# Routed experts after attention: scatters straight from six input tiles at ten a turn, expert codes counted once from a table, and fresh units from batch 13

## The reference, cut to what matters

```
x = x + cross_attention(layernorm(x), ctx)            # 16 heads of 8
z = layernorm(x)
scores = sigmoid(z @ gate_w.T) + gate_bias            # 64 experts in 8 groups
keep the 4 groups with the largest maxima, then the 6 largest scores, weights divided by their sum
routed = sum over the 6 of weight * down_e(silu(gate_e(z)) * up_e(z))     # inner width 64
shared = one expert of inner width 128, for every token
out = x + shared + routed
```

## Time and profile before

| what | value |
|---|---|
| runs | 802.83, 805.97, 804.34 us |
| span of the profiled execution | 792.4 us |
| median of the runs less that span | 11.9 us (launch and end; the profiled execution's own time is not listed) |
| PE busy | 503.3 us, 64% |
| DVE busy | 456.1 us, 58% |
| POOL busy | 389.3 us, 49% |
| ACT busy | 352.3 us, 44% |
| granted PE clock, mean | 0.675 of full speed |

### The profile page before, as it was taken

The page is one execution under the profiler, slowest core; times in us unless marked ns, Lnnn a source line. Parts: engine busy times, 40 slices in busy tenths (PEclk is TensorE's granted clock), DMA queues, the critical chain, the costliest instruction groups (busy, mean ns, idle before and its releaser), DMA issues.

```text
span 792.4 us, 12061 instructions
## 1 busy us (share of the span) xinstructions
PE 503.3 (64%) x3204; PEld 420.8 (53%) x3204; DVE 456.1 (58%) x2264; ACT 352.3 (44%) x962; POOL 389.3 (49%) x425
## 2 busy tenths in 40 slices
PE   3767555766555574632359956788688889777700
PEld 2445334444334343311359856778688789777700
DVE  6587556667555576656233624576776756346532
ACT  3564433344443343322215934466666766246400
POOL 2006445654455655556650055454554545555574
PEclk9885555555555555555568976899988876897555
DMA  7532123322123332223425533455455555654421
GB/s 195 194 113 94 62 100 107 104 100 98 47 80 107 107 100 98 95 78 129 124 81 134 148 94 95 106 138 151 126 145 137 151 137 146 160 153 107 113 70 47
DMA packets 98708, 90.60 MB, mean 114 GB/s; under 512 B 10576, under 2 KB 85456, under 8 KB 98640
## 3 DMA queue, kind: packets, MB, share of 16 engines
q1 hardware_dynamic: 85232, 64.26, 27.5%
q0 software_dynamic: 12288, 25.29, 11.3%
q10 hardware_dynamic: 1120, 0.28, 0.2%
HBM read 41.32 MB, written 48.46 MB: 113 GB/s over the span
## 4 chain that ended last, share of the span: by engine, by line
PE 30%; another core or an unknown queue 17%; issue 16%; ACT 14%; POOL 11%; DVE 9%; ACTq 2%; DMA 0%; POOLq 0%; DVEq 0%
PE bank_s L1155 14%; POOL pages L447 6%; PE bank_o L1155 4%; PE bank_q L1155 3%; PE bank_s L1151 2%; ACT d_now L511 2%; ACT p_t L533 2%; ACT pxt L511 2%; POOL empty L492 2%; ACT gu_now L511 2%; ACT k_exp L521 1%; ACT s_act L672 1%; POOL p_t L492 1%; PE bank_o L1151 1%
## 5 line engine op out<-in xcount | busy, mean ns | idle before, releaser
L1155 PE MATMUL bank_s<-pxt,gu_now 128*128 128x64 f32 x768 | 116.5, 316 | 51.6 <-ACT pxt L511 31.3
L492 POOL DMA_INDIRECT p_t<-results,place_i x96 | 91.1, 949 | 110.6 <-ACT s_act L672 72.8
L1155 PEld LDWEIGHTS bank_s<-pxt,gu_now 128*128 128x128 f32 x768 | 111.4, 231 | 58.1 <-ACT pxt L511 36.4
L492 POOL DMA_INDIRECT empty<-results,place_i x96 | 91.1, 949 | 77.2 <-issue 35.1
L1111 DVE TENSOR_TENSOR h_t<-bank_s,s_act 64x256 f32<-64x256 f32 x128 | 54.7, 427 | 113.9 <-ACT s_act L672 95.4
L447 POOL DMA_INDIRECT pages<-payload,place_i x96 | 93.0, 968 | 37.9 <-issue 27.0
L447 POOL DMA_INDIRECT pages<-payload_b,place_i x96 | 92.8, 967 | 35.8 <-issue 26.7
L437 POOL TENSOR_TENSOR rstd<-ve,minus_half 128x4 f32<-128x4 f32 (+1 forms) x21 | 18.6, 885 | 132.6 <-DVE ve L927 130.0
L672 ACT ACTIVATE s_act<-bank_s 64x512 f32<-64x512 f32 x64 | 37.8, 590 | 79.5 <-remote 36.0
L533 ACT ACTIVATE p_t<-bank_s 128x512 f32<-128x512 f32 x64 | 36.2, 598 | 67.9 <-issue 27.9
L1255 PE MATMUL bank_o<-bias_h,row_h 96*128 96x256 bf16 x16 | 6.1, 381 | 72.2 <-ACT o_t L511 70.3
(11 more groups left out here) (169 smaller groups left out, 1164.1 us busy)
## 6 DMA issues: line engine op xcount, KB each, us to landing
pg<-pages SPq DMA_DIRECT2D x64, 258.0 KB
results<-y_s SPq DMA_DIRECT2D x64, 256.0 KB
pages<-empty SPq DMA_DIRECT2D x21, 774.0 KB
w_gu<-in_expert_gu SPq DMA_DIRECT2D x16, 256.0 KB
w_d<-in_expert_d SPq DMA_DIRECT2D x31, 128.0 KB
out_x<-xb SPq DMA_DIRECT2D x16, 128.0 KB
xb<-in_x SPq DMA_DIRECT2D x3, 512.0 KB, 8.0
pages<-payload,place_i POOLq DMA_INDIRECT x96
```

The lines of the kernel that those rows point to most:

```text
L492: pool.indirect_dma_start(out=ys[n % YS_SLOTS][:, k, :], out_offset=None, in_=results[0:landed * QUAD * P, :], in_offset=bass.IndirectOffs ...
L1155: return pe.matmul(dst, w, v, start=True, stop=True)
```

## The change

- **Scatters.** `payload`, `fill_payload` and the expert's number in a row are gone; pages have rows of 128 numbers. There are six `xn2` tiles in place of two, and POOL scatters straight from them. ACT, before it writes a tile again, waits for the scatters of six batches before. A turn of POOL now issues ten scatters and then `rstd`; `sent_by(b)` = 10(b-2)-5 says how many are out after turn b. So five go in turn 3, 155 are out after turn 18, and 37 follow with nothing between.
- **Places.** In place of twelve picks and two conversions a batch: `is_expert` (bf16, 768 elements in a partition, inside `find_rows`), one product `picked` and one sum to integers, each over both tiles.
- **Experts of the units.** `next_page` is kept for all batches. In quad 0 DVE's `count_units` finds the expert of every unit with nine chained operations, PE packs them with four small matmuls at quad 2 (`pack_codes`), DVE keeps them at quad 3 (`keep_codes`), and registers are loaded from that table. `pack_experts` and SP's wait for it are gone.
- **Fresh units.** `SPLIT` = 13: the first section has 47 quads and needs 156 scatters, the second has 17 quads. Both sections have DRAM tensors of their own for pages and for results. `PLACE_STEPS` goes from 30 to 19.

```diff
-SPLIT = B - 2
+SPLIT = B - 3
+XN2_SLOTS = 6
+A_BATCH = TPB * TOPK
+SENT_A_TURN = 10
+HELD_BACK = 5
...
+            def scatter(n, t, k):
+                if t == 0 and k == 0:
+                    pool.wait_ge(place_ready, n + 1)
+                    pool.wait_ge(xn2_ready, TPB * (n + 1))
+                    pool.wait_ge(prefilled, 16 * fills_before(n))
+                pool.indirect_dma_start(out=(new_pages if n >= SPLIT else old_pages)[:, :], out_offset=bass.IndirectOffsetOnAxis(
+                    ap=place_i[:, TPB * n + t, k:k + 1], axis=0), in_=xn2[n % XN2_SLOTS][:, t, :],
+                    in_offset=None).then_inc(scattered[n % XN2_SLOTS], 16)
+
+            def sent_by(b):
+
+                return max(0, SENT_A_TURN * (b - 2) - HELD_BACK)
...
+            for b in range(FIRST_BODY - 1, BODIES_END):
+                scatters(sent_by(b - 1), sent_by(b))
                 if any_norm(b + 1):
                     inverse_deviations(b + 1)
...
+            scatters(sent_by(BODIES_END - 1), B * A_BATCH)
...
             def normalise_x2(n, side):
-                if n >= 2:
-                    act.wait_ge(payload_x, TPB * (n - 1))
-                normalise(n, TPB, xn2[side], side, n + 2, xn2_ready)
+                if n >= XN2_SLOTS:
+                    act.wait_ge(scattered[n % XN2_SLOTS], 16 * A_BATCH * (n // XN2_SLOTS))
+                normalise(n, TPB, xn2[n % XN2_SLOTS], side, n + 2, xn2_ready)
...
-            def fill_payload(n, side, t):
-                act.wait_ge(xn2_ready, TPB * n + t + 1)
-                act.wait_ge(scattered[n % 2][t], 16 * TOPK * (n // 2))
-                copy(payload[n % 2][:, t, :, 0:D], xn2[side][:, t, :].unsqueeze(1).to_broadcast([P, TOPK, D])).then_inc(payload_x, 1)
...
+                chained("is_expert", dve.tensor_tensor(
+                    is_expert[:, :, :, :], iota_h[:, :].unsqueeze(1).unsqueeze(1).to_broadcast([P, TPB, TOPK, E]),
+                    experts(expert_h[:, :, :]), ALU.is_equal))
...
+                place_step(n, "pick", dve.tensor_tensor(picked[:, :, :, :], is_expert[:, :, :, :],
+                                                        row[:, :, :].unsqueeze(2).to_broadcast([P, TPB, TOPK, E]), ALU.mult))
...
+                    dve.tensor_reduce(place_i[:, TPB * n:TPB * (n + 1), :], picked[:, :, :, :], AX.X, ALU.add).then_inc(place_ready, 1)
...
+            def count_units():
+
+                for c in range(UNIT_TILES + 1):
+                    batches, tile = (slice(0, SPLIT), c) if c < UNIT_TILES else (slice(SPLIT, B), 0)
+                    size = batches.stop - batches.start
+                    if c > 0:
+                        dve.wait_ge(counted, 2 * c)
+                    dve.scalar_tensor_tensor(out=at_or_under[:, 0:size, :], in0=next_page[:, batches, :], scalar=unit[:, tile:tile + 1],
+                                             in1=ones_e[:, :].unsqueeze(1).to_broadcast([P, size, E]), op0=ALU.is_le, op1=ALU.mult,
+                                             accum_out=opened_by[:, c:c + 1]).then_inc(counted, 1)
...
+            def pack_codes():
+                pe.wait_ge(counted, 2 * (UNIT_TILES + 1) + 1)
+                pe.wait_ge(sh_added, SHARED_FIRST)
+                pe.wait_ge(digits_made, QUAD)
+                for c in range(UNIT_TILES + 1):
+                    last = mm(bank_w[0:1, c * CODES:(c + 1) * CODES], unit_expert[:, c:c + 1], digits[:, :, :].rearrange("p q h -> p (q h)"))
+                last.then_inc(codes_done, 1)
```

More of the change, by code:

```diff
@@ L68 @@
 SHARED_FIRST = 2
+CODES_AT = 2
 SHARED_AT = FIRST_SUM - 3
@@ L163, in build @@
         o_t = sb("o_t", [P, TOK])
-        xn2 = [sb(f"xn2_{i}", [P, TPB, D]) for i in range(2)]
+        xn2 = [sb(f"xn2_{i}", [P, TPB, D]) for i in range(XN2_SLOTS)]
         sig = sb("sig", [P, TPB, E])
@@ L437, in inverse_deviations @@
                 pool.tensor_tensor(rstd[b % 2][:, part], ve[:, part], minus_half[:, part], ALU.pow).then_inc(rstd_done, 1)
-            def wait_payload(n, t):
-                pool.wait_ge(place_ready, TPB * n + t + 1)
-                pool.wait_ge(payload_x, TPB * n + t + 1)
-                pool.wait_ge(prefilled, 16 * fills_before(n))
-            def scatter(n, t, first, after):
-                wait_payload(n, t)
-                for k in range(first, after):
-                    pool.indirect_dma_start(out=pages[:, :], out_offset=bass.IndirectOffsetOnAxis(
-                        ap=place_i[:, TPB * n + t, k:k + 1], axis=0), in_=payload[n % 2][:, t, k, :],
-                        in_offset=None).then_inc(scattered[n % 2][t], 16)
@@ L460, in body, with scatters @@
+            def sent_by(b):
+                return max(0, SENT_A_TURN * (b - 2) - HELD_BACK)
+            def scatters(first, after):
+                for i in range(first, after):
+                    n, place = divmod(i, A_BATCH)
+                    scatter(n, place // TOPK, place % TOPK)
+            for b in range(FIRST_BODY - 1, BODIES_END):
+                scatters(sent_by(b - 1), sent_by(b))
                 if any_norm(b + 1):
                     inverse_deviations(b + 1)
-                if on(n):
-                    if ahead < TOPK:
-                        scatter(n, 0, ahead, TOPK)
-                    if ahead < 2 * TOPK:
-                        scatter(n, 1, max(0, ahead - TOPK), TOPK)
@@ L468, in _ @@
-            for b in range(FIRST_BODY - 1, BODIES_END):
-                body(b)
+            scatters(sent_by(BODIES_END - 1), B * A_BATCH)
             def beat(step):
@@ L1104, in quad @@
             def quad(q):
-                if q + 2 < NQ and held(q + 2) is None:
-                    pack_experts(q + 2)
                 dve.wait_ge(act_ready, q + 1)
@@ L1176, in transpose_x2 @@
             def transpose_x2(n):
-                side = n % 2
                 pe.wait_ge(xn2_ready, TPB * (n + 1))
                 pe.wait_ge(ranks_ready, n)
-                transposes([bank_r[:, t * P:(t + 1) * P] for t in range(TPB)], [xn2[side][:, t, :] for t in range(TPB)], x2t_done)
+                transposes([bank_r[:, t * P:(t + 1) * P] for t in range(TPB)], [xn2[n % XN2_SLOTS][:, t, :] for t in range(TPB)], x2t_done)
             def logits(n):
@@ L1412 @@
     args.append(nc.dram_tensor("out_x", (B, TOK, D), F32, kind="ExternalOutput").ap())
-    args.append(nc.dram_tensor("pages", (PAGES * P, PC), F32, kind="Internal").ap())
-    args.append(nc.dram_tensor("results", (PAGES * P, D), F32, kind="Internal").ap())
+    args += [nc.dram_tensor(f"{age}_{what}", (n * P, D), F32, kind="Internal").ap()
+             for what in ("pages", "results") for age, n in (("old", OLD_PAGES), ("new", NEW_PAGES))]
     build(nc, *args)
```

217 lines of the change are left out of this document (117 added, 100 removed).

## The result

The changed kernel takes 782.64 us (median of 4 runs, 781.31 to 784.06), the kernel before 803.59 (4 runs, 802.59 to 805.97): ratio 0.974, 95% interval 0.970 to 0.979. The forecast was 795.0 us with a range of 783 to 809: the sign was right, the gain of 21 us was more than twice the 9 us that it gave, and the time lies 0.4 us under the range. The profiled execution of the changed kernel took 782.59 us with a span of 780.8, so 1.8 us lie around the span.

What follows compares the result with a forecast made beforehand. Stage 1 turns were taken as bound by POOL's scatter burst delaying PE's completions (1.2 + 12 x 1.27 + 2.3 + 5.0 = 23.7 us). Span 792.4 - 9.5 = 782.9, with 11.9 around it: 795 us, range 783 to 809.

Steps and rivals of the forecast that it cites:

- no hold at all: Rival, 5 in 100: turns keep 23.46 us, quads run at 3.44 us under the scatters, quad 3 gains 1 us; 803 us.
- The other turns look the same: Stage 1: all turns were taken to resemble the one read, with `sig` and `q_t` coming only after the last scatter's end.
- Ten a turn: Stage 1: ten scatters a turn for twelve save 2.54 us each; with turns 3 and 16, -34.3 us together.
- The slower rival: Rival, 13 in 100: another wait bounds the turn, turns keep up to 23.46 us, quad 3 comes 24 us later; 828 us.
- `q_t` still some 2.3 us behind each burst: Sign in the profile after: in stage 1 turns `q_t` would still follow each burst of ten by some 2.3 us.
- Places: DVE, stage 1: twelve picks a batch become three operations of 0.97 us, hidden in DVE's 7.16 us wait; nothing gained.
- Payload copies: ACT, stage 1: removing two copies of 0.84 us a turn gains nothing; bounds 0 and -0.8 us a turn.
- Setup: Before the first norm: digits, a cast, two memsets and an iota add 0.9 us, at most 2.0.
- Quads under the burst: Stage 2 start: 2.8 quads pass at 11.9 us each before the release; quad 3 near 412, -9.5 us (bounds -17, -1).
- the long burst stops PE: Rival, 13 in 100: quad 1 stands at 411 us and the gain is only 1 to 2 us; 803 us.
- Counting the units: Quad 0: about 5 us on DVE, covered by a 10 us quad; +5 us if the cover went.
- SPLIT, the quads after, the tail: Stage 2: batch 13's gathers find their results ready, later quads keep their spacing (0 to -5 us), the 46.98 us tail stays.

## Why the prediction was right and wrong

- **The bound and the mechanism: right.** The chain runs through PE completions that a stream of indirect DMAs holds; pauses alone take turns of 23.46 us to 19.0. The rival "no hold at all" wanted turns of 23.46 us and a time of 803, and no run agrees with it. That is the time by the rule of the Trainium skill, "SBUF — State Buffer", section "Who interferes with whom" ("PE and ACT never wait on anyone"); the section speaks of the ports of SBUF, and no run here shows that the hold has to do with those. "The other turns look the same" was true of `q_t` (1.8 to 2.4 us behind the burst in the ten turns) and not of `sig`, which in four of them came 2 to 3 us before the burst's end.
- **Ten a turn: right.** -33.0 us forecast for the turns from 4 on, -30.7 measured (twelve against ten, all else equal). The slower rival, a turn that isn't the burst's, is out.
- **"`q_t` still some 2.3 us behind each burst": wrong.** It came before the burst's end; `o_t` came 1.5 us behind it.
- **Places: the first failed step.** "The difference falls in front of the 7.16 us for which DVE waits: nothing." The three operations took 0.95, 0.90 and 0.94 us as forecast, and DVE's wait did cover the work. But the term was worth -25 us by turn 17, for the most part through the release of the logits in the middle of the burst. I had checked which work was covered, and not what else moves when its timing does. `rstd` of turn 17 came at 314.63 and not 335.4.
- **Payload copies: right** (nothing, 19.26 against 19.2 us).
- **Setup: mis-sized.** +0.9 forecast; `rstd` of turn 4 stands 2.2 us later in this profile, though in others of the changed kernel it stands at 68.8.
- **The burst of 57: right,** 73.8 us from `rstd` to its end for 73.0 forecast.
- **Quads under the burst: the second failed step.** "From 377 to the release at 408.4 + 2.3 quads crawl", at 11.9 us each. From the real `rstd` the same working gives quad 0 at 356.2 and quad 3 at about 391. Quad 0 came at 394.97: nothing passed for some 40 us, and the release came 6.6 us behind the burst's end, not 2.3. I priced a burst of 57 by quads with six to nine DMAs, and gave the rival "the long burst stops PE" 13 in 100. It happened, in this profile from quad 0 on and in others from quad 1. That quad 3 stood at 408.48 for 412 is luck: the two errors nearly cancelled. The rows of before had the sign of it. I took 8.5 us from the first page to quad 0's `s_act` "with a burst running", but POOL stood idle there:

```profile
391.34 0.96 POOL L447 DMA_INDIRECT pages<-payload,place_i  x1 [0.30 <-issue]
399.41 0.96 POOL L447 DMA_INDIRECT pages<-payload_b,place_i  x1 [7.10 <-DVE place_i L886]
```

Quad 0's `s_act`, at 395.83, came in this break of 7.10 us, 3.5 us behind the end of the DMA before it. Only quad 1 (406.40) passed under a stream, 7 us after that stream had begun.
- **Counting the units: the work right, the cover not.** DVE took 5.1 us for it (397.18 to 402.28), as forecast; but with the burst over quad 1's `s_act` came 5.8 us behind quad 0's and not 10, so `h_t` of quad 1 waited for the counting, until 402.32, about 1 us.
- **SPLIT, the quads after, the tail: right** in sum, 325.5 us from quad 3 to the last quad for 324.0 before, and a tail of 46.8. That SPLIT brings quad 0 forward was right and worth nothing.
- **The sum: the third failed step, and the largest in the total.** The forecast span was 782.9, the profiled one 780.8. "The median of the runs lies 11.9 above its span, and I keep that" added 10.1 us that no execution has; 2.1 + 10.1 are the 12.2 us by which the sum, 794.8 before rounding, was off. Of the measured 21 us, 11.6 are the difference of the first two profiles, and the rest is how much shorter the profiled execution of before was than its usual ones. Why it was shorter stays open.

## What to carry to other kernels

Where POOL issues indirect DMAs back to back, look for consumers of PE that idle on something unnamed, and break the stream with about a microsecond of other work every three or four DMAs: each such break cost POOL 0.9 us (2.19 us from one DMA to the next in place of 1.27), and together they gave 8% here with nothing else changed. Put scatters that nobody needs at once behind the steps of the stage they run under, not in one burst ahead of it (0.955 of the time of before, where the changed kernel takes 0.974). And when a span is far from the median, find out what lies around a span before adding the difference to a forecast.

## What the runs showed of the hardware that I had not expected

- PE's completions were held for up to some 40 us while indirect DMAs stood 1.27 us apart, as in the row of the chain with 39.48 us above. In the runs with one unbroken burst of 57 the release came 4.7 to 8.6 us behind its end; in the turns of the kernel before `q_t` came 1.8 to 2.4 us behind a burst of twelve. It was PE's completions alone as far as the turn shown of the changed kernel tells: there DVE took `sig` from ACT 0.03 us after its end, with the burst still running.
- It goes with the stream of DMAs and not with its bytes: rows of 128 bytes held quad 1 for 35 us like rows of 512. It is not POOL's being busy: fills of 1.06 or 2.84 us let completions through. 0.49 us between two DMA instructions was too short a break, 1.23 us was enough. Every run on record lists a span and a clock, so each seems to have been recorded by the profiler; whether the hold is there without that, no run tells.
- An indirect DMA instruction of POOL that started while DVE's `is_expert` or `picked` (768 elements) ran took longer than 0.96 us: 1.12 and 1.44 us in the turn shown of the changed kernel, 1.64 us in one of the run with pauses in the turns (139.79). Beside the sum of 768 elements (`place_i`) and the picks of 64 elements it stayed at 0.96 or 0.97.
